# Queries and keys of all blocks but the first as three products of split operands

## What is computed

```python
xn = (x - mean(x)) / sqrt(var(x) + 1e-5)        # layernorm over the 256 features
Q = xn @ Wq.T + bq ; K = xn @ Wk.T + bk ; V = xn @ Wv.T + bv      # 16 heads of 16
A = softmax(Q @ K.T / 4)                         # per batch and head, 2048 x 2048
x = x + ((0.6 * A + 0.4 * local_band) @ V) @ Wo.T + bo
x = x + moe(layernorm(x))                        # router, top 2 of 4 experts, hidden size 1024
```

## Time and profile before

| | |
|---|---|
| median of 3 runs | 2013.65 us (2012.37 to 2017.76) |
| the profiled execution, its own time | 2025.48 us |
| its span, first to last instruction | 2023.7 us |
| busy in the span: PE, DVE, ACT, POOL | 97%, 80%, 68%, 17% |
| mean granted TensorE clock | 0.989 |
| project (last low piece done) | about 78 us of the span |

### The profile page before, as it was taken

One profiled execution on the slowest core, in us unless ns is written; L12 is line 12 of the kernel. 1 busy time (PEld: TensorE's weight loads), 2 busy tenths in 40 slices (PEclk: granted clock), 3 DMA queues, 4 the chain that ended last, 5 costly groups with the idle time before them and its releaser, 6 DMA issues. The chain is left out here.

```text
span 2023.7 us, 48037 instructions
## 1 busy us (share of the span) xinstructions
PE 1972.7 (97%) x16480; PEld 1051.8 (52%) x16480; DVE 1621.5 (80%) x2035; ACT 1374.0 (68%) x2471; POOL 347.4 (17%) x379
## 2 busy tenths in 40 slices
PE   7999999999999999999999999999999899999997
PEld 4543333333333333333333333333687689999996
DVE  6779999999999999999999999994255565555554
ACT  3338888888888888888888888889544422222331
POOL 1370001000100010001000100010024532232233
PEclk9979999999999999999999999999999899999999
DMA  7935335433543355335533553341122777788884
GB/s 268 243 81 114 74 84 118 91 73 79 121 93 73 76 112 105 73 74 107 112 73 74 105 114 73 73 97 49 42 76 87 286 228 238 241 256 302 256 267 111
DMA packets 105849, 264.09 MB, mean 130 GB/s; under 512 B 20896, under 2 KB 52768, under 8 KB 99104
## 3 DMA queue, kind: packets, MB, share of 16 engines
q1 hardware_dynamic: 92624, 245.29, 45.2%
q0 software_dynamic: 13152, 17.83, 4.5%
HBM read 206.95 MB, written 73.94 MB: 139 GB/s over the span
## 5 line engine op out<-in xcount | busy, mean ns | idle before, releaser
L619 DVE TENSOR_REDUCE part_max<-psum 128x1 f32<-128x1024 f32 x1024 | 1241.9, 1222 | 59.5 <-PE psum L741 47.0
L674 ACT ACTIVATE probs<-psum 128x512 f32<-128x512 f32 x2048 | 1111.1, 596 | 153.2 <-PE psum L754 86.1
L754 PE MATMUL psum<-score_q,score_k 50*128 50x512 f32 x2048 | 749.5, 448 | 1.2 <-DMA score_q<-shift_row 1.2
L741 PE MATMUL psum<-max_k,max_q 48*128 48x512 f32 x2048 | 742.4, 451 | 1.2 <-DVE part_max L619 1.1
L766 PE MATMUL psum<-probs,v_ones 128*32 128x256 f32 x8192 | 658.0, 393 | 9.4 <-ACT heads_sb L689 9.0
L754 PEld LDWEIGHTS psum<-score_q,score_k 50*128 50x128 f32 x2048 | 308.6, 186 | 408.6 <-ACT probs L674 394.0
L766 PEld LDWEIGHTS psum<-probs,v_ones 128*32 128x32 f32 x8192 | 162.5, 108 | 383.3 <-issue 200.8
L741 PEld LDWEIGHTS psum<-max_k,max_q 48*128 48x128 f32 x2048 | 296.0, 186 | 13.9 <-issue 7.5
L1159 ACT ACTIVATE x_sb<-psum,x_sb 128x512 f32<-128x512 f32 (+1 forms) x160 | 101.4, 635 | 260.0 <-PE psum L1520 253.4
L1539 PE MATMUL psum<-w,h_hi 128*128 128x256 f32 x1120 | 204.9, 280 | 0.6 <-issue 0.3
L1539 PEld LDWEIGHTS psum<-w,h_hi 128*128 128x128 f32 x1120 | 180.0, 189 | 11.6 <-issue 0.5
(11 more groups left out here) (179 smaller groups left out, 1367.7 us busy)
## 6 DMA issues: line engine op xcount, KB each, us to landing
w<-w_split SPq DMA_DIRECT2D x40, 2048.0 KB
max_q<-qk_pieces SPq DMA_DIRECT2D x192, 128.0 KB, 7.4
score_k<-qk_pieces SPq DMA_DIRECT2D x192, 128.0 KB, 4.6
xs<-in_pads SPq DMA_DIRECT2D x33, 528.0 KB, 5.9
qk_pieces<-pieces SPq DMA_DIRECT2D x32, 512.0 KB, 4.7
w_split<-w_pair SPq DMA_DIRECT2D x32, 512.0 KB, 6.6
max_k<-qk_pieces SPq DMA_DIRECT2D x192, 64.0 KB, 7.4
score_q<-qk_pieces SPq DMA_DIRECT2D x192, 64.0 KB, 2.2
```

What stands on the lines that cost most here:

```text
L619: nc.vector.tensor_reduce(part_max[:, t, p:p + 1], ps_m[p].rearrange("q b f -> q (b f)"), axis=AXIS.X, op=ALU.max).then_inc(m_read, 1)
L674: nc.scalar.activation(probs[kb % 2][:, chunk * BLOCK:(chunk + 1) * BLOCK], bank_of(at), ACT.Exp, scale=float(HD) ** -0.5).then_inc(exp_do ...
L741: last = nc.tensor.matmul(ps_m[p][:, h, :], max_q[u][rows, t * P:(t + 1) * P], max_k[u][rows, p * BLOCK:(p + 1) * BLOCK], start=True, stop ...
L754: nc.tensor.matmul(bank_of(at), score_k[u][rows, kb * P:(kb + 1) * P], score_q[u][rows, part * BLOCK:(part + 1) * BLOCK], start=True, stop ...
```

## The change

For all blocks but block 0, q and k come from three products of fp32r operands, high x high, high x low and low x high, in six matmuls per bank in place of two fp32 ones. POOL makes the splits: once `w_q` and `w_k`, and per block the transposed rows (`split_xT`, two buffers). On PE the transposes of block n+1 move ahead of all matmuls of block n. On ACT `copy_T` of block n+1 moves ahead of the first bank copy of block n. In POOL's list the inversion for block n+1 stands ahead of the split of block n.

```diff
--- before.py
+++ after.py
@@ -162,6 +162,8 @@
     x_sb, v_sb, ident, max_q, max_k = (keep[n] for n in ("x", "v", "ident", "max_q0", "max_k0"))
     w = {"q": sb("w_q", [P, KD, DIM]), "k": sb("w_k", [P, KD, DIM]), "v": keep["w_v"]}
     bias_v, xnT = keep["bias_v"], keep["xnT"]
+    w_hi, w_lo = ({n: sb(f"w_{n}_{piece}", [P, KD, DIM], F32R) for n in "qk"} for piece in ("hi", "lo"))
+    xT_hi, xT_lo = ([sb(f"xnT_{piece}{u}", [P, KD, BLOCK], F32R) for u in range(2)] for piece in ("hi", "lo"))
     bias_qk = sb("bias_qk", [P, 2, KD])
     half = sb("half", [P, BT])
     stats = [sb(f"stats{u}", [P, BT, 6]) for u in range(2)]
@@ -181,6 +183,7 @@
 
     stats_done, mv_done, var_ready, rstd_ready = sem("stats_done"), sem("mv_done"), sem("var_ready"), sem("rstd_ready")
     xn_ready, t_ready, xnT_ready = sem("xn_ready"), sem("t_ready"), keep["xnT_ready"]
+    w_split, xT_split_hi, xT_split = sem("w_qk_split"), sem("xnT_split_hi"), sem("xnT_split")
     qk_ready, piece_hi, piece_lo = sem("qk_ready"), sem("piece_hi"), keep["piece_lo"]
     stored, first_stack = keep["stored"], keep["first_stack"]
     pairs = BLOCKS // 2
@@ -240,10 +243,35 @@
         nc.gpsimd.memset(v_sb[:, :, 0], 0.0).then_inc(pool_set, 1)
         nc.gpsimd.memset(v_sb[:, :, ST + 1], 0.0).then_inc(pool_set, 1)
         pool.wait_ge(pool_set, 3)
-        with pool.Fori(0, pairs) as i:
-            for u in range(2):
-                pool.wait_ge(var_ready, 2 * i + u + 1)
-                nc.gpsimd.tensor_tensor(rstd[u][:], var[u][:], half[:], ALU.pow).then_inc(rstd_ready, 1)
+
+        def invert(n, u):
+            pool.wait_ge(var_ready, n + 1)
+            nc.gpsimd.tensor_tensor(rstd[u][:], var[u][:], half[:], ALU.pow).then_inc(rstd_ready, 1)
+
+        def split_w(n, done):
+            nc.gpsimd.tensor_copy(w_hi[n][:], w[n][:]).then_inc(w_split, 1)
+            pool.wait_ge(w_split, done + 1)
+            nc.gpsimd.tensor_tensor(w_lo[n][:], w[n][:], w_hi[n][:].bitcast(F32), ALU.subtract).then_inc(w_split, 1)
+
+        def split_xT(n, u):
+
+            pool.wait_ge(xnT_ready, n + 1)
+            if n >= 3:
+                pool.wait_ge(qk_ready, QK * (n - 1))
+            block = xnT[:, n, :, :]
+            nc.gpsimd.tensor_copy(xT_hi[u][:], block).then_inc(xT_split_hi, 1)
+            pool.wait_ge(xT_split_hi, n)
+            nc.gpsimd.tensor_tensor(xT_lo[u][:], block, xT_hi[u][:].bitcast(F32), ALU.subtract).then_inc(xT_split, 1)
+
+        invert(0, 0)
+        invert(1, 1)
+        pool.wait_ge(weights_in, 16 * 2)
+        split_w("q", 0)
+        split_w("k", 2)
+        for n in range(1, BLOCKS):
+            if n + 1 < BLOCKS:
+                invert(n + 1, (n + 1) % 2)
+            split_xT(n, n % 2)
 
     @block.vector
     def _(dve):
@@ -316,7 +344,7 @@
                     act.wait_ge(stored[u], 16 * QK * i)
 
                 for j in range(QK):
-                    if j == KD and not (last and u):
+                    if j == 0 and not (last and u):
                         copy_T(n + 1)
                     act.wait_ge(qk_ready, QK * n + j + 1)
                     nc.scalar.activation(pieces[u][:, j // KD, j % KD, 0, :], ps_qk[j], ACT.Identity,
@@ -343,18 +371,29 @@
         def body(i, first, last):
             for u in range(2):
                 n = 2 * i + u
-                pe.wait_ge(xnT_ready, n + 1)
+                if not (last and u):
+                    transposes(n + 1, 1 - u)
+
+                whole = first and u == 0
+                if whole:
+                    pe.wait_ge(xnT_ready, 1)
+                else:
+                    if first:
+                        pe.wait_ge(w_split, 2 * 2)
+                    pe.wait_ge(xT_split, n)
                 for qk in range(2):
-                    if qk == 1 and not (last and u):
-                        transposes(n + 1, 1 - u)
+                    name = "qk"[qk]
                     for m in range(KD):
-                        j = 2 * qk + m
-                        if not (first and u == 0):
+                        j, feats = 2 * qk + m, slice(m * P, (m + 1) * P)
+                        if not whole:
                             pe.wait_ge(piece_lo, QK * (n - 1) + j + 1)
-                        for k in range(KD):
-                            done = nc.tensor.matmul(ps_qk[j], w["qk"[qk]][:, k, m * P:(m + 1) * P],
-                                                    xnT[:, ds(n, 1), k, :].squeeze(1),
-                                                    start=k == 0, stop=k == KD - 1)
+                        if whole:
+                            terms = [(w[name][:, k, feats], xnT[:, ds(n, 1), k, :].squeeze(1)) for k in range(KD)]
+                        else:
+                            terms = [(ws[name][:, k, feats], xs[u][:, k, :])
+                                     for ws, xs in ((w_hi, xT_hi), (w_hi, xT_lo), (w_lo, xT_hi)) for k in range(KD)]
+                        for t, (stationary, moving) in enumerate(terms):
+                            done = nc.tensor.matmul(ps_qk[j], stationary, moving, start=t == 0, stop=t == len(terms) - 1)
                         done.then_inc(qk_ready, 1)
 
         peeled(pe, body)
```

## The result

The changed kernel takes 2153.04 us (median of 4 runs, 2151.24 to 2158.51) where the kernel before takes 2013.81: ratio 1.068, 95% interval 1.0648 to 1.0713. It is 139 us slower. The prediction was 2013.0, with 2008 to 2020.5 as its range.

What follows compares the result with a forecast made beforehand. Project was taken as PE-bound, then bound by a 7.05 us loop in place of 7.74. Block 0's 1.2 us cost left 1.0 gained by block 3; stores cut that to 0.7: 2013.65 - 0.7 = 2013.0, range 2008 to 2020.5.

Steps and rivals of the forecast that it cites:

- a shift of everything behind it: After project: stages behind it have no changed line, so a gain in project only moves them, no more.
- The PE terms: Project, per block: 24 fp32r matmuls at 0.231 take 5.54 us in place of 6.87; with transposes 6.4 for 7.74.
- Block 0: Start of project: block 1's transposes now precede its fp32 matmuls, so it ends at 24.5, not 23.3; cost 1.2 us.
- The weight splits: POOL, about 12.4 to 16.5 us: two casts and two subtractions, 4 us, free beside PE's slow start.
- POOL's split: POOL, per block in project: a cast and a subtraction of 1024 elements, 3.5 us.
- The loop of 7.05 us: Project, new bound: statistics, inversion, split, then PE's matmuls; 7.05 us per block in place of 7.74.
- POOL and DVE shut each other out: Rival in project, chance 0.12: normalise waits for the whole split, 8.2 us per block, 2015.2 us in all.
- the normalise's pace, 0.33 us per 256 elements: Sign from DVE in project: same pace as the statistics' 0.35, so no mode with two elements at a time.
- The stores: End of project: ACT waits for stores until 65.6, delaying block 7's copy and split; first maxima 77.7, total gain 0.7 us.
- the idle spell ahead of block 7: End of project: PE, done with block 6 at 66.8, idles until 70.3, waiting 3.5 us for block 7's split.
- that clock rival: Rival, chance 0.32: PE's 3.5 us wait ahead of block 7 lowers the clock; 2016 if short, 2023.4 if long.
- Chances: Whole kernel: 0.75 within 6 us of 2013.65, 0.07 faster, 0.18 slower, of which 0.17 for a long low-clock spell.

Runs made afterwards that it cites:

- order_only: The changed kernel's new order on PE and ACT alone, with plain fp32 matmuls and no splits; 2017.93 us, ratio 1.0008 to the kernel before.
- splits_unused: The changed kernel's order and POOL splits, but PE multiplies plain fp32 rows and waits for no split; 2025.96 us, ratio 1.0035 to the kernel before.
- split_held: Changed kernel with 40 tiny matmuls ahead; POOL starts a block's split only after DVE normalised the next block; 2021.69 us, ratio 1.0009.
- split_quarters: Changed kernel with 40 tiny matmuls ahead and each of POOL's two split instructions per block cut in four; 2024.98 us, ratio 1.0054.
- act_norm: Changed kernel with 40 tiny matmuls ahead, normalise of blocks 2 to 7 on ACT, copy_T before the store wait; 2020.89 us, ratio 1.0026.

## Why the prediction was wrong, point by point

- **"What follows ... not one line of it is changed; I take a gain in project as a shift of everything behind it."** This step failed, with 123.6 of the 125.7 us. The lines are the same, the addresses are not. 72 more instructions ahead moved a loop of 6.8 blocks from 7 blocks onto 8, and from then on each jump back cost 9 transfers, a gap of 2.7 us, and about 16 us at half clock behind it, which lose some 7. Nothing in the profile of before announces it directly, but two things were there to be counted: 44 instruction transfers over 2023.7 us, too few for a loop of seven blocks to be fetched anew in 15 turns, and the length of that loop. The Trainium skill, Runtime: NRT & Kernel Launch, "Instruction fetch mechanics", says that PE's instruction memory holds 2048 instructions and is refilled in blocks of 256, and that a taken branch whose target is not in the current two-page window stalls for a fetch. I had not brought it to bear. The runs agree on the blocks and on the stall. They do not agree on the window: a loop on 7 blocks jumps back without one (11 transfers within attend), and only one on 8 does not stay.
- **The PE terms**: right. 46.96 - 46.50 = 0.46 for two, as in the earlier trace rows.
- **Block 0**: wrong in both terms. For the order alone I took 1.2 us; `order_only` shows 0.1, because its matmuls, started at 15.89, took only 4.1 us for the first eight records (15.89 to 19.95), where they took 6.25 before. The weight splits, which I took for free, cost the rest: in the changed kernel the transposes began at 16.51 and not at 13.9, because the normalise of block 1 took 3.98 us next to them, and block 0 ended at 26.8, not 24.5.
- **POOL's split**: right, 40.74 to 44.25, 3.5 us.
- **The loop of 7.05 us**: wrong, 9.3. The loop that I took as the bound was not the bound; DVE's loop, which I had at 6.8 and hidden, grew by the 2.6 us that the normalise lost, and became it. PE then waits at the transposes for the normalise, and not for the split. This was the rival "POOL and DVE shut each other out", to which I gave 0.12. I read the normalise's pace, 0.33 us per 256 elements, as a sign against it. That inference was wrong: the normalise is held up in spite of its pace. The rule of the Trainium skill (SBUF — State Buffer, "SBUF: two separate sides") that I had weighed agrees with the runs: `splits_unused` and `split_held` for the normalise, `split_quarters` for "the whole instruction", and `act_norm` for an instruction with two SBUF inputs, which that section names too. That the normalise runs in a two-port mode no row shows by itself. My price for it, 8.2 per block, was still too low, since I priced the loop through the split and not DVE's own: 2.1 statistics, 0.7 first low piece, 4.1 normalise, 2.1 three low pieces, 0.3 waiting.
- **The stores**: the wait is where I said, ACT 5.1 us up to 76.17, with `copy_T` behind it. But all of it came 10 us late, and block 6 on PE ended only at 80.9, when the split of block 7 was done. So the idle spell ahead of block 7 did not come, and with it that clock rival. The clock did fall in project behind other gaps, of 2.6 to 2.8 us: the transposes at 35.86 and 73.00 took 1.97 us, and the matmuls at 55.92 had a pitch of 0.43. Even without splits the stores landed at 69.08, not at 65.6 (`order_only`).
- **Chances**: slower had 0.18, nearly all of it on one mechanism with a price of up to 10 us. A gap of some 3 us followed by many us of half clock was the right picture, at a place I did not look at and 14 times over.

## What to carry to other kernels

A change that alters the number of instructions ahead of a long loop changes the loop. Before forecasting "the rest only shifts", count the loop's instructions in blocks, see from the instruction transfers whether it is fetched anew in each turn, and ask how many more instructions move it over an edge; filling a few dozen instructions into a stretch in which the engine is idle tests it in one run and repairs it. And before giving POOL elementwise work next to DVE, lay the two timelines side by side: here DVE lost as long as POOL's instruction lasted, and delaying POOL (`split_held`) was 7 us better than starting it at once.

## What I had not expected of the hardware

- PE's loop of 1736 instructions runs without transfers when it touches 7 blocks of 256 (44 or 45 transfers in the whole program), and with about 127 more, 9 per jump back, when it touches 8. The gap per turn was 2.7 us (72 added), 3.0 (40 added), 3.9 (20 added), and 6.8 in two parts (196 added).
- By the positions of the compiled list 3, 23, 27 and 247 into a block are fast, and 47, 67, 99 and 223 slow. This fits if the code begins 10 to 29 instructions further into a block than the list says; the start itself was not seen.
- A semaphore increment on PE takes 0.15 us; a fp32 matmul of 4 x 4, four instructions, 2.15 / 40 = 0.05 us.
- Two DVE instructions wait for POOL's to end: fp32 `tensor_scalar` on SBUF (2.56 us for one at the longest, median 0.41) and a `scalar_tensor_tensor` with two SBUF inputs. The statistics (1.41 us at 52.10 of `split_held`, next to a subtraction until 52.92) and the low piece, which reads PSUM (0.75 at 51.38), kept their times.
